# Two mixtures' routing decided inside the self-attention stage ahead of each

## The chip, the cores and the metric

The kernel runs as one program on one core of a Trainium2 chip. Its engines are TensorE (PE, matmul; PEld is its weight load), VectorE (DVE), ScalarE (ACT), GpSimd (POOL) and SyncE (SP, which issues transfers). The metric is the time of one execution in microseconds; lower is better.

## The reference, cut to what matters

A stream `x` of 128 sequences of 32 tokens and 128 channels (4096 tokens, 32 tiles of 128 tokens) passes twelve residual layers. Layers 4 and 5 are a cross-attention and a causal self-attention, layer 6 a mixture of 8 experts with two experts a token and a capacity of 1280 tokens an expert; layer 11 is a causal self-attention with rotary places and layer 12 begins with a second one of its kind and ends in a mixture with one expert a token. For each mixture:

```
logits = norm(x) @ W_router                 # 8 numbers a token
top1   = argmax(logits)                     # or the two best, with softmax weights
u      = norm(x) @ W1[top1] + b1            # GELU with four blocks, or a gated form with two
y      = act(u) @ W2[top1] + b2
x      = x + weight * y                     # weight 0 where the expert is over its capacity
```

What is computed stays the same in the change.

## The kernel before, in words

`X` stays in SBUF as [128, 32 tiles, 128]. The stages run one after another, each a block with a barrier at its end; inside a block each engine has its own ordered list of instructions, and semaphores order them against each other. Three stages are mixtures (`routed_experts`): `a_moe`, `c_moe` (two experts, capacity, four blocks) and `u_moe` (one expert, gated). Before `c_moe` runs `c_self` (`self_attention` with two parts of 32 tiles, so 64 steps), before `u_moe` runs `u_self` (32 steps, rotary, a gate), and after `c_moe` the cross-attention `e_cross`.

**A self-attention** is a software pipeline over steps, one tile a step. `chunk_at(s, place)` says at which step a piece of work for four tiles (a chunk) is due: queries, keys and values before the chunk's first tile, `outputs` at place 7, `output` at 8, the addition onto the stream at 9. Each engine goes through its own list of one step in a fixed order: PE `scores(s)`, projections, `weighted(s-2)`, `turn(s-1)`; DVE `maximum(s)`, `subtract(s)`, `reciprocals`, `unit`; ACT `exponential(s)`, `turned(s-1)`, `apply(s+APPLY)`; POOL `heads(s+2)` and the small arithmetic of the norm (`deviation`). The loop runs to step ALL_TILES + 5.

**A mixture** begins with its front. It cuts the 32 tiles in two halves of 16. DVE takes statistics, POOL the deviation, ACT writes the normed rows (`apply`), PE turns them and forms the logits, DVE chooses experts (`choose`), PE counts with two matmuls, DVE forms each token's row in a buffer sorted by expert (`places`), and POOL scatters every tile's rows to that buffer in DRAM with one indirect DMA a tile and expert (`put(0)`: 32 transfers in `c_moe`, 16 in `u_moe`). Only when the first half is put does SP load sorted tiles (`load`), three at a time, which PE turns (`turn_x`). PE also waits for both halves' owners and, in `c_moe`, for the ranks against the capacity (`s_chosen`); in `u_moe` DVE first adds all of `inner` onto `X`. Then comes the loop over COUNT sorted tiles (78 in `c_moe`, 48 in `u_moe`), each with one expert's weights picked by a register: `up`, activation, `turn_hidden`, `hidden_out`, `down`, `result`. The second half's transfers (`put(1)`) run beside it, one a tile, and the first half's results are fetched back by POOL and added by DVE (`combine`). In `c_moe` the second half's 32 results are fetched in the first 16 tiles of `e_cross` (`fetch_result`, `add_result`).

## Time and profile before

| | us |
|---|---|
| median of 3 runs (lowest, highest) | 4168.02 (4163.99, 4170.11) |
| profiled execution, its own time | 4170.86 |
| profiled execution, span of the trace | 4169.1 |

| stage of the trace | from, us | to, us |
|---|---|---|
| c_self | 1756.7 | 1959.2 |
| c_moe, to the first sorted tile on PE | 1959.5 | 2044.9 |
| c_moe, loop | 2044.9 | 2250.1 |
| e_cross | 2252.7 | 2795.5 |
| u_self | 3779.0 | 3991.5 |
| u_moe, to the first hidden tile on PE | 3991.8 | 4048.5 |
| u_moe, loop and fetching | 4048.5 | 4162.3 |

Times of the trace count from the start of its span. The columns of each view are said at the first group of its rows. A busy share is an average over a stretch: which wait ends last in the stretch is read from the instructions in order of time.

### The profile page before, as it was taken

Reading aid. Unit: us, or ns where it says so; the run is one execution under the profiler, and the core shown is the slowest. Engines: PE = TensorE matmul, PEld = TensorE weight load, DVE = VectorE, ACT = ScalarE, POOL = GpSimd, SP = SyncE. Lnnn points to the kernel's source line nnn. Section 1 sums busy time; section 2 is a strip of 40 time slices with the busy share of each in tenths; the row PEclk is TensorE's granted clock in tenths of the full one; section 3 lists DMA queues with packets and bytes.
Section 4 is the critical chain, followed back from the end, with each engine's and each line's share of the span. In section 5 each row is a group of like instructions: output and inputs, shape, how many; then the busy total and the mean of one; then the engine's idle time right before and its main releaser. Section 6 shows DMA issues by size and latency. Waiting matters only on the chain. (4 is left out here: it accounts for less than half of the span.)

```text
span 4169.1 us, 119554 instructions
## 1 busy us (share of the span) xinstructions
PE 3506.7 (84%) x44673; PEld 2455.7 (59%) x44674; DVE 2783.9 (67%) x6958; ACT 2401.5 (58%) x5931; POOL 2497.3 (60%) x2841
## 2 busy tenths in 40 slices
PE   7999959999999669698598899978589999786766
PEld 5666637777677447465366666655356666453444
DVE  6888856666666423476445998876778888763655
ACT  6777735555555334286123777764567777543633
POOL 6666657767666553475424777655456666755733
PEclk9999979999999779898699999998689999887968
DMA  2111010000000122101121111110011111000023
GB/s 70 35 35 38 27 67 5 7 10 10 6 7 2 51 63 80 50 17 43 51 72 59 46 40 36 38 62 3 2 43 32 38 32 33 2 2 6 2 85 93
DMA packets 90544, 145.87 MB, mean 35 GB/s; under 512 B 10112, under 2 KB 66816, under 8 KB 89664
## 3 DMA queue, kind: packets, MB, share of 16 engines
q1 hardware_dynamic: 79936, 119.72, 8.9%
q0 software_dynamic: 10240, 20.99, 1.6%
q8 instruction: 261, 4.28, 0.4%
q14 instruction: 107, 0.88, 0.1%
HBM read 109.61 MB, written 31.06 MB: 34 GB/s over the span
## 5 line engine op out<-in xcount | busy, mean ns | idle before, releaser
L2230 POOL TENSOR_TENSOR t_cross_E<-t_cross_E,t_cross_inverse 128x1028 f32<-128x1028 f32 x128 | 243.4, 1902 | 164.0 <-DVE t_cross_inverse L2512 164.0
L2230 POOL TENSOR_TENSOR a_cross_E<-a_cross_E,a_cross_inverse 128x1028 f32<-128x1028 f32 x128 | 243.3, 1901 | 157.1 <-DVE a_cross_inverse L2512 157.1
L2230 POOL TENSOR_TENSOR e_cross_E<-e_cross_E,e_cross_inverse 128x1028 f32<-128x1028 f32 x128 | 243.6, 1903 | 137.1 <-DVE e_cross_inverse L2512 136.6
L3063 PE MATMUL l_psum<-l_ffn_w,l_hidden 128*128 128x128 f32 x1536 | 214.9, 284 | 3.0 <-POOL l_hidden L2936 3.0
L3063 PEld LDWEIGHTS l_psum<-l_ffn_w,l_hidden 128*128 128x128 f32 x1536 | 192.3, 193 | 29.9 <-issue 22.2
L3056 PE MATMUL l_psum<-l_hT,l_ffn_w 128*128 128x512 f32 x384 | 204.1, 634 | 0.9 <-ACT l_hT L3120 0.9
L2500 DVE TENSOR_REDUCE t_cross_negtop<-t_cross_psum 128x2 f32<-128x514 f32 x256 | 165.5, 688 | 48.9 <-PE t_cross_psum L2314 47.4
L2500 DVE TENSOR_REDUCE a_cross_negtop<-a_cross_psum 128x2 f32<-128x514 f32 x256 | 165.2, 687 | 40.9 <-PE a_cross_psum L2309 40.4
L2500 DVE TENSOR_REDUCE e_cross_negtop<-e_cross_psum 128x2 f32<-128x514 f32 x256 | 164.9, 685 | 36.5 <-PE e_cross_psum L2309 35.8
L2915 POOL TENSOR_SCALAR l_normed<-inner,l_moments,l_rstd 128x128 f32<-128x128 f32 x192 | 175.6, 924 | 14.8 <-POOL l_rstd L2909 14.8
L3219 DVE TENSOR_TENSOR inner<-l_psum,inner 128x512 f32<-128x512 f32 x48 | 33.2, 692 | 213.0 <-PE l_psum L3048 213.0
L3040 PEld LDWEIGHTS l_psum<-l_qT,l_ctx 32*32 32x32 f32 x6144 | 66.9, 107 | 148.0 <-issue 142.4
L2926 POOL TENSOR_TENSOR l_q<-l_q,l_q_stat 128x512 f32<-128x512 f32 x48 | 50.9, 1060 | 168.6 <-DVE l_q_stat L3199 168.6
L2367 PE MATMUL e_cross_psum<-const_sb,e_cross_E 128*128 128x128 f32 x1024 | 134.0, 274 | 2.7 <-POOL e_cross_E L2230 2.1
L2367 PE MATMUL a_cross_psum<-const_sb,a_cross_E 128*128 128x128 f32 x1024 | 133.7, 274 | 2.2 <-POOL a_cross_E L2230 2.1
L2367 PE MATMUL t_cross_psum<-const_sb,t_cross_E 128*128 128x128 f32 x1024 | 132.8, 273 | 2.1 <-POOL t_cross_E L2230 2.1
L2936 POOL TENSOR_TENSOR l_hidden<-l_hidden,l_less 128x512 f32<-128x512 f32 x96 | 123.1, 1301 | 18.4 <-ACT l_hidden L3144 18.4
L2435 ACT ACTIVATE t_cross_kT<-t_cross_psum,t_cross_weights 128x257 f32<-128x257 f32 x128 | 61.0, 477 | 126.2 <-PE t_cross_psum L2293 126.2
L2435 ACT ACTIVATE e_cross_kT<-e_cross_psum,e_cross_weights 128x257 f32<-128x257 f32 x128 | 61.0, 477 | 121.8 <-PE e_cross_psum L2293 121.8
L2435 ACT ACTIVATE a_cross_kT<-a_cross_psum,a_cross_weights 128x257 f32<-128x257 f32 x128 | 61.0, 477 | 120.5 <-PE a_cross_psum L2293 120.5
L2452 ACT ACTIVATE e_cross_E<-e_cross_psum,e_cross_negtop 128x257 f32<-128x257 f32 x256 | 118.8, 473 | 13.4 <-DVE e_cross_negtop L2500 13.1
L1491 POOL DMA_INDIRECT slots<-hT_all,behind_place_i x64 | 62.0, 968 | 96.6 <-PE c_moe_psum L1623 72.4
(757 smaller groups left out, 11855.6 us busy)
## 6 DMA issues: line engine op xcount, KB each, us to landing
a_cross_context<-context SPq DMA_DIRECT2D x32, 546.0 KB, 3.5
e_cross_context<-context SPq DMA_DIRECT2D x32, 546.0 KB, 3.5
t_cross_context<-context SPq DMA_DIRECT2D x32, 546.0 KB, 3.5
u_moe_weights<-pack_u_moe SPq DMA_DIRECT2D x1, 5633.0 KB
slots<-l_blank SPq DMA_DIRECT2D x6, 832.0 KB, 12.2
a_moe_x_slots<-slots SPq DMA_DIRECT2D x26, 192.0 KB
slots<-a_moe_y_slots SPq DMA_DIRECT2D x26, 192.0 KB
c_moe_x_slots<-slots SPq DMA_DIRECT2D x26, 192.0 KB
```

Source lines behind the costliest of these rows:

```text
L1491: pool.indirect_dma_start(slots.halves[g], bass.IndirectOffsetOnAxis(ap=place_i[:, k, at:at + 1], axis=0), rows[:, at], None).then_inc(s_p ...
L2230: pool.tensor_tensor(E[:, n % N], E[:, n % N], spread(inverse[:, n % 4], SK, 2), ALU.mult).then_inc(s_unit, 1)
L2367: last = pe.transpose(psum[:, (T_BANK, K_BANK)[c], g * P:(g + 1) * P], E[:, n % N, g, c * P:(c + 1) * P], ident)
L2435: act.activation(kT[:, n % 2], psum[:, K_BANK, 0:SK], ACT.Identity, bias=w("bk")).then_inc(s_k, 1)
L2452: act.activation(E[:, n % N, g], psum[:, g, 0:SK], ACT.Exp, bias=negtop[:, n % 2, g:g + 1], accum_out=total[:, n % 2, g:g + 1]).then_inc(s ...
L2500: dve.tensor_reduce(negtop[:, n % 2, at], psum[:, at, 0:SK], AX.X, ALU.max, negate=True).then_inc(s_top, 1)
L2915: last = pool.tensor_scalar(Y1[:, t], c.tile(t), moments[:, 0, t, 0:1], rstd[:, 0, 1, t:t + 1], ALU.subtract, ALU.mult)
L2926: pool.tensor_tensor(groups, groups, spread(q_stat[:, 2], DH, 2), ALU.mult).then_inc(s_soft, 1)
L2936: pool.tensor_tensor(hidden[:, f], hidden[:, f], less[:, f - 2], ALU.add).then_inc(s_late, 1)
L3040: last = pe.matmul(psum[rows, C_BANK, b * S:(b + 1) * S], ctx[rows, b], qT[rows, b * S:(b + 1) * S], start=True, stop=True)
L3056: pe.matmul(psum[:, U_BANKS[f % 2]], c.ffn(f * P), hT2[:], start=True, stop=True).then_inc(s_up, 1)
L3063: last = pe.matmul(psum[:, D_BANK, t * P:(t + 1) * P], hidden[:, f, t * P:(t + 1) * P], c.ffn((NF + f) * P), start=(f == 0 and t == 0), st ...
```

## The change

- The mixture's front becomes two classes: `Choice` (its buffers) and `Front` (its work in pieces, each called by an engine). `self_attention` takes a `choice` and calls the pieces at places 9 (statistics), 10 (deviation), 11 (apply), 13 (turn) and 14 (logits) for chunks 0 to 6; chunk 7 stays in the mixture's stage. The loop of steps goes on to ALL_TILES + 9.
- The first part's choice is made on DVE at steps CHOOSE.. (54, 55 in `c_self`; 26 in `u_self`), the counts on PE at TALLY (57; 28), the places on DVE in three steps from TALLY.
- From step PUT (61; 30) POOL issues one scatter transfer a step: 9 of `c_moe`'s and 8 of `u_moe`'s. The mixture's stage opens with the others.
- The first part of `c_moe` is 12 tiles and not 16 (24 transfers), the second 20 (40 transfers). With the rounding of parts to triples the loop has 81 tiles, not 78. `u_moe` keeps 16 and 16, and 48. `e_cross` fetches 40 results, not 32, over 20 tiles.
- Chunk 7's front, the second part's choice, counts and places, the ranks against the capacity, the weights of the two experts and the addition of `inner` (in 8 pieces) go between the tiles of the mixture's loop. PE no longer waits for `s_chosen`.
- The second part's transfers wait for `s_down` at a pace set so that they end 6 tiles before the first part does.
- Router and expert weights are fetched in the self-attention. The owners' registers are loaded at tile 13 of 16, not 2. `base(c)` on POOL moves from place 5 to place 1 in every self-attention.
- `a_moe` keeps its front in its stage, through the new classes.

```diff
@@ self_attention
+        F_STATS, F_DEVIATION, F_APPLY, F_TURN, F_LOGITS = 9, 10, 11, 13, 14
+        if choice:
+            front = Front(sc, choice, 0, 0)
+            CHOOSE = (ALL_CHUNKS - CHUNKS) * TPC + choice.cut[1] - TPC + F_LOGITS
+            TALLY = CHOOSE + choice.K + 1
+            PUT = max(TALLY + 2, ALL_TILES - 3)
+            choice.ahead_of_stage = ALL_TILES + 6 - PUT
-            for s in range(-STATS, ALL_TILES + 6):
+            for s in range(-STATS, ALL_TILES + (10 if choice else 6)):
@@ POOL, step
-                c = chunk_at(s, 5)
+                c = chunk_at(s, 1)
                 if c is not None:
                     base(c)
+                c = fronted(s, F_DEVIATION)
+                if c is not None:
+                    front.deviation(pool, link, c)
+                if choice and PUT <= s < ALL_TILES + 6:
+                    if s == PUT:
+                        pool.wait_ge(front.s_place, 1)
+                    front.put(pool, slots, 0, s - PUT)
@@ PE, step (after scores and projections, before weighted(s - 2))
+                c = fronted(s, F_TURN)
+                if c is not None:
+                    turned_free(s)
+                    front.turn(pe, c, psum[:, T_BANK])
+                c = fronted(s, F_LOGITS)
+                if c is not None:
+                    front.arrived(pe)
+                    outputs_free(s)
+                    ...
+                    front.logits(pe, c, psum[:, O_BANK, LOGITS])
+                if choice and s == TALLY:
+                    front.tallies(pe, 0, psum[:, O_BANK, TALLIES])
@@ PE, turn(s)
+                c = fronted(s + 1, F_TURN)
+                if c is not None:
+                    pe.wait_ge(front.s_fT, c + 1)
@@ ACT, step (rotary: before powers(c), normed_out(c) and exponential(s))
+                c = fronted(s, F_TURN)
+                if c is not None and rotary:
+                    front.turned(act, c, psum[:, T_BANK])
@@ DVE, step
+                c = fronted(s, F_LOGITS)
+                    ...
+                    front.read_logits(dve, (c,), psum[:, O_BANK, LOGITS])
+                if choice and s == TALLY:
+                    front.places(dve, link, 0, 0, psum[:, O_BANK, TALLIES])
                 if tile_exists(s - 2):
                     unit(s - 2)
+                if choice and 0 <= s - CHOOSE < choice.K:
+                    front.choose(dve, link, 0, s - CHOOSE)
+                if choice and 0 < s - TALLY < 3:
+                    front.places(dve, link, 0, s - TALLY, psum[:, O_BANK, TALLIES])
+                c = fronted(s, F_STATS)
+                    ...
+                    front.statistics(dve, c)
@@ Choice
+        self.cut = 0, first, TILES
+        self.triples = [-(-(self.K * (self.cut[g + 1] - self.cut[g]) + self.E - 1) // 3) for g in range(2)]
@@ routed_experts, POOL
+                    if g == 1:
+                        pool.wait_ge(s_down, PUT_AT + n * (ONE - 6 - PUT_AT) // transfers if begun else n + 1)
+            if begun:
+                for n in range(choice.ahead_of_stage, choice.width(0) * K):
+                    front.put(pool, slots, 0, n)
+                front.deviation(pool, link, LAST)
@@ routed_experts, DVE
+            def beside(i):
+                if i == 2:
+                    front.read_logits(dve, (LAST,), psum[:, COUNT_BANK, 0:TPC * E])
+                if 2 <= i < 2 + K:
+                    front.choose(dve, link, 1, i - 2)
+                if 0 <= i - PLACES_AT < 3:
+                    front.places(dve, link, 1, i - PLACES_AT, psum[:, COUNT_BANK, TPC * E:])
+                ...
+                if capacity and 0 <= i - RANK_AT - 2 < 2 * RANKING:
+                    ranking(*divmod(i - RANK_AT - 2, RANKING))
+                if base is not None and 0 <= i - RANK_AT < CHUNKS:
+                    add_base(i - RANK_AT)
@@ fourth, second_self
+                choice = Choice(sc, "u_router", "top1", inner, hT_rows, "eps6", rms=True)
+                choice = Choice(sc, "c_router", "capacity", X, hT_rows, "eps5", affine=False, first=12)
```

## Rows read from the trace of the kernel before

**Rows 1.** By stretch: PE, PEld, DVE, ACT, POOL busy; TensorE clock, DMA share, GB/s.
```profile
1860.00:1945.00 85.00, 81.41 (x2306) 51.74 (x2306) 68.18 (x180) 70.60 (x132) 61.08 (x76) 1.00 0.02 4
...
1959.50:2045.00 85.50, 25.46 (x113) 23.63 (x114) 40.12 (x172) 17.15 (x41) 44.02 (x64) 0.54 0.22 83
...
3910.00:3975.00 65.00, 52.76 (x1139) 30.28 (x1138) 42.89 (x83) 42.68 (x66) 40.46 (x40) 0.95 0.01 3
...
3991.80:4048.00 56.20, 27.96 (x111) 23.54 (x111) 29.08 (x128) 17.88 (x43) 25.48 (x32) 0.50 0.36 139
4048.00:4137.00 89.00, 83.28 (x421) 55.39 (x421) 62.61 (x158) 41.00 (x111) 30.55 (x32) 0.97 0.28 82
```

**Rows 2.** In order of time, c_moe's front: start, us, what [idle before <-releaser].
```profile
1958.49 0.69 DVE L793 TENSOR_TENSOR X<-c_self_psum,X 128x512 f32<-128x512 f32 x1 [3.09 <-PE c_self_psum L552]
...
2030.09 0.96 POOL L1491 DMA_INDIRECT slots<-hT_all,behind_place_i  x1 [0.30 <-issue]
...
2032.34 13.86 SPq L1433 DMA_DIRECT2D c_moe_x_slots<-slots  x5
...
2044.93 0.87 PE L1592 MATMUL c_moe_psum<-const_sb,c_moe_x_slots 128*128 128x128 f32 x3 [19.15 <-issue]
```

**Rows 3.** The first sorted tiles in a_moe: ns min/median/max, first and last start us.
```profile
L1592 PE MATMUL a_moe_psum<-const_sb,a_moe_x_slots x78: 272/273/476, 1504.9 to 1686.4; 128*128 128x128 f32 x78
L1433 SPq DMA_DIRECT2D a_moe_x_slots<-slots x26: 360/488/1055, 1502.5 to 1665.2; - x26
```

**Rows 4.** In order of time, u_moe's front.
```profile
3990.81 0.69 DVE L793 TENSOR_TENSOR inner<-u_self_psum,inner 128x512 f32<-128x512 f32 x1 [2.17 <-PE u_self_psum L552]
...
4042.31 0.88 PE L1592 MATMUL u_moe_psum<-const_sb,u_moe_x_slots 128*128 128x128 f32 x3 [6.23 <-issue]
...
4040.89 4.42 DVE L1837 TENSOR_TENSOR X<-X,inner 128x4096 f32<-128x4096 f32 x1
...
4048.52 0.69 PE L1614 MATMUL u_moe_psum<-const_sb,u_moe_hidden 128*128 128x128 f32 x2 [0.62 <-DVE u_moe_hidden L1880]
```

**Rows 5.** In order of time, PE: two chunks of c_self, and c_moe's logits.
```profile
1906.56 1.16 PE L552 MATMUL c_self_psum<-c_self_weights,c_self_aT 128*128 128x128 f32 x8
...
1917.60 1.16 PE L552 MATMUL c_self_psum<-c_self_weights,c_self_aT 128*128 128x128 f32 x8
...
1967.17 1.72 PE L1530 MATMUL c_moe_psum<-c_moe_router,c_moe_fT 128*128 128x8 f32 x8
```

**Rows 6.** In order of time, DVE: choice's first, places' first and last instruction.
```profile
1976.29 0.29 DVE L1317 TENSOR_REDUCE c_moe_best<-c_moe_l 128x16 f32<-128x128 f32 x1
...
1982.17 0.29 DVE L1777 COPY c_moe_counts<-c_moe_psum 128x128 f32<-128x128 f32 x1 [1.37 <-PE c_moe_psum L1544]
...
1987.91 0.18 DVE L1796 CAST c_moe_owner_i<-c_moe_owner 128x39 int32<-128x39 f32 x1
```

**Rows 7.** In order of time, c_moe's loop: PE three tiles apart, DVE between two tiles.
```profile
2100.73 1.02 PE L1606 MATMUL c_moe_psum<-c_moe_weights,c_moe_xT 128*128 x2
...
2108.22 1.02 PE L1606 MATMUL c_moe_psum<-c_moe_weights,c_moe_xT 128*128 x2
...
2105.47 0.29 DVE L1897 COPY c_moe_y_slots<-c_moe_psum 128x128 f32<-128x128 f32 x1 [1.36 <-PE c_moe_psum L1623]
```

**Rows 8.** In order of time, u_self: ACT's load for a chunk's powers, PE's `turn_normed`.
```profile
3939.81 1.28 ACT L641 ACT_TABLE_LOAD   x1
...
3939.69 0.66 PE L467 MATMUL u_self_psum<-const_sb,u_self_normed 128*128 128x128 f32 x4
```

**Rows 9.** Adding a fetched result: ns min/median/max, in c_moe and in e_cross.
```profile
L1907 DVE SCALAR_TENSOR_TENSOR X<-behind_got,behind_part,X x32: 342/344/344, 2167.5 to 2245.9; 128x128 f32<-128x128 f32 x32
L2554 DVE SCALAR_TENSOR_TENSOR X<-behind_got,behind_part,X x32: 962/1388/1998, 2283.2 to 2543.3; 128x128 f32<-128x128 f32 x32
```

**Rows 10.** Busy time of POOL's work on e_cross_E, with fetches and without.
```profile
2300.00:2400.00 100.00, 46.64 (x31) 1.00 0.13 41
...
2640.00:2740.00 100.00, 49.69 (x32) 1.00 0.13 39
```

More of the change, by code:

```diff
@@ L336, in _ @@
                 fetch(sp)
+            if choice:
+                front.fetch(sp)
             for c in range(ALL_CHUNKS):
@@ L680, in step @@
                         work(c)
+                c = fronted(s, F_TURN)
+                if c is not None:
+                    front.turned(act, c, psum[:, T_BANK])
                 if tile_exists(s):
@@ L836, in step @@
                             rotate(c, n)
+            link = Link(dve, front.s_link, 0) if choice else None
             steps(step)
@@ L1345, in routed_experts @@
-def routed_experts(core, name, router, rows, slots, kind, choice, nf, source, eps, rms=False, twice=False, capacity=None,
-                   base=None, hT_all=None, store_out=None, behind=None):
-    nc, X = core.nc, core.X
-    E, K, HALF = 8, (1 if choice == "top1" else 2), TILES // 2
-    NT = core.half_tiles[K]
-    TRIPLES = -(-NT // 3)
-    COUNT, LOT = 2 * 3 * TRIPLES, 16
-    halves = kind in ("silu", "glu")
-    width = nf * P * (2 if halves else 1)
+        self.s_put, self.puts = [ctx.enter_context(nc.semaphore(f"put{g}")) for g in range(2)], [0, 0]
@@ new lines, in __init__, with routed_experts @@
+        self.s_got, self.gots = [ctx.enter_context(nc.semaphore(f"got{n}")) for n in range(4)], 0
+def routed_experts(core, name, slots, kind, nf, choice, begun=False, base=None, store_out=None, behind=False):
+    nc, X = core.nc, core.X
+    E, K, cut, rows, hT_all = choice.E, choice.K, choice.cut, choice.rows, choice.hT_all
+    TRIPLES, COUNT, LOT = sum(choice.triples), choice.count, 16
+    ONE = 3 * choice.triples[0]
+    capacity = 1280 if choice.kind == "capacity" else None
+    width = nf * P * (2 if kind in ("silu", "glu") else 1)
@@ L1394, in routed_experts @@
+        front = Front(sc, choice, LAST, 1) if begun else Front(sc, choice, 0, 0)
+        w, arrived, fetch = sc.weights(choice.expert if begun else name)
+        ex = sc.sb("ex", [P, TILES])
+        if capacity:
+            rank1, rank2, tot, tot_b = [sc.sb(n, [P, TILES, E]) for n in ("rank1", "rank2", "tot", "tot_b")]
         x_slots, xT = sc.sb("x_slots", [P, 4, 3, P]), sc.sb("xT", [P, 2, 3 * P])
@@ L1494, in take @@
-            def take(g):
-                stores_done(pool, (g + 1) * TRIPLES)
-                for t in range(HALF):
-                    for k in range(K):
-                        at = g * HALF + t
-                        n = at * K + k
+            link = Link(pool, front.s_dev, 0)
+            def put(g):
+                pool.wait_ge(front.s_place, g - front.g0 + 1)
+                transfers = choice.width(g) * K
+                for n in range(transfers):
+                    if g == 0 and n in (4 * K, 8 * K):
+                        front.deviation(pool, link, PART + 1 + n // (4 * K))
+                    if g == 1:
+                        pool.wait_ge(s_down, PUT_AT + n * (ONE - 6 - PUT_AT) // transfers if begun else n + 1)
+                    front.put(pool, slots, g, n)
@@ L1500, in take @@
+            def take(g):
+                stores_done(pool, choice.triples[0] + g * choice.triples[1])
+                for t in range(cut[g], cut[g + 1]):
+                    for k in range(K):
+                        n = t * K + k
                         if n >= 4:
@@ L1539, in _, with ranks @@
                         turn(c + 1)
-                    choose(c)
-                pe.wait_ge(s_mask, g + 1)
-                mask = flat((one if K == 1 else p8)[:, of(g)])
-                for n, table in enumerate(("upto", "ones")):
-                    last = pe.matmul(psum[:, COUNT_BANK + g, n * P:(n + 1) * P], core.const(table), mask, start=True, stop=True)
-                last.then_inc(s_count, 1)
-            if choice == "capacity":
-                for k, chosen in enumerate((one, two)):
+                    at = c % PART * TPC * E
+                    front.logits(pe, c, psum[:, LOGIT_BANK + g, at:at + TPC * E])
+                front.tallies(pe, g, psum[:, COUNT_BANK + g])
+            arrived(pe)
+            def ranks():
+                for k, chosen in enumerate((choice.one, choice.two)):
                     for n, table in enumerate(("upto", "ones")):
@@ L1580, in load_owners @@
                 if first < last:
+                    if begun and first < ONE < last:
+                        pe.wait_ge(front.s_owner, 1)
                     at = lot % 2 * LOT
@@ L1629, in _ @@
             up(0)
+            if begun:
+                front.turn(pe, LAST, psum[:, RANK_BANK])
             for i in range(COUNT):
@@ L1723, in _ @@
                     hidden_out(i)
+                if begun and i == 0:
+                    front.turned(act, LAST, psum[:, RANK_BANK])
+                if begun and K == 2 and i == RANK_AT:
+                    ratios()
             if shared:
@@ L1814, in _, with apart @@
[L1814 to L1826 removed]
+            def apart():
+                dve.tensor_tensor(ex[:], choice.v2[:], choice.v1[:], ALU.subtract).then_inc(s_apart, 1)
@@ L1857, in load_owners @@
                 if first < last:
+                    if begun and first < ONE < last:
+                        dve.wait_ge(front.s_owner, 1)
                     at = lot % 2 * LOT
@@ L1903, in combine @@
                     dve.wait_ge(s_comb, n)
+                elif n == 0 and base is not None:
+                    dve.wait_ge(s_base, CHUNKS)
                 if K == 1:
```

642 lines of the change are left out of this document (382 added, 260 removed).

## The prediction

> **What bounds the kernel now.** I read the busy shares by stretch first. The reader is to see that no engine is the bound of the whole: PE is busy 96% of a stretch of c_self (81.41 of 85.00) and 81% of one of u_self, but 30% in c_moe's front and 50% in u_moe's, where its clock also falls to about half [rows 1]. In these two fronts the instructions in order of time tell what is waited for. c_moe's lasts from the last addition of c_self (1958.49 + 0.69 = 1959.2) to the first sorted tile on PE at 2044.93: 85.7 us [rows 2]. POOL issues 32 scatter transfers in it, each 0.96 with 0.30 ahead of it, so 1.26; the last ends at 2031.05 [rows 2], and the rest are the ranks, which PE waits for. u_moe's lasts from 3991.5 to the first hidden tile at 4048.52: 57.0 us, with 16 transfers and at its end the 4.42 of DVE's addition of `inner` [rows 4]. The loops behind them run without gaps on PE: three tiles of c_moe take 2108.22 - 2100.73 = 7.49 us [rows 7]. So the fronts are worth 142.7 us together, and what is put in other stages lands where PE or a ring of engines is full.
>
> **What goes.** c_moe's stage opens with 24 - 9 = 15 transfers: 14 x 1.26 + 0.96 = 18.6. SP's load followed the last of them by 1.3 (2032.34 against 2031.05) [rows 2], and in a_moe, where PE waits for nothing else, the first tile came 2.4 after that load (1504.9 against 1502.5) [rows 3]. With 0.5 for the barrier: 22.8, so 62.9 go. u_moe's opens with 16 - 8 = 8: 7 x 1.26 + 0.96 = 9.8, in all 14.0 to the first tile on PE. From there to the first hidden tile it was 6.2 (4042.31 to 4048.52) with DVE held by the addition until 4045.3 [rows 4]; without it, but with chunk 7's rows ahead on ACT, I take 5.2. 57.0 - 19.2 = 37.8 go. **Gain: 100.7.**
>
> **What comes into c_self.** PE gets for each of chunks 0 to 6 four transposes (about 0.44) and eight matmuls for the logits. Eight matmuls of the shape took 1.72 at half clock; eight of 128 columns take 1.16 at the full one, 0.99 to the next [rows 5], so I take 0.9. Two chunks of that place stand 11.04 apart on a full PE [rows 5]; five front chunks fall there, two in the tail. To the 1.3 I add 0.5, because `turn(s-1)` now waits until ACT has emptied the bank: 5 x 1.8 = 9. Bounds: 5 (only the matmuls, and some in idle PE time) and 13.5 (a whole step of 2.7 each). Choice and places on DVE took from 1976.29 to 1988.09 with 1.4 of waiting for PE between them, 10.4 for 16 tiles [rows 6]; for 12 with a copy more I take 9.7, over five steps in which DVE idles 0.2 of 2.76 each [rows 1], so 2.7 hide: 7 stay (0 to 9.7). The tail: chunk 6's rows wait for the addition of chunk 6, POOL's deviation, ACT, PE, and end after chunk 7's output; and POOL's nine transfers and the clearing of semaphores, once done long before the end, end there too. I take 5 (2 to 8). POOL's queue: the transfers begin after the last `heads` is issued, so no tile waits for them; the deviation (1.7) stands ahead of a later `heads`, which POOL issues two steps early (5.5 us): nothing. If that lead is used up, the next scores are late by the rest.
>
> **DVE beside POOL.** One row speaks against putting a choice beside busy POOL: adding a fetched result takes 0.34 in c_moe's loop, where POOL issues transfers, and 0.96 to 2.00, median 1.39, in e_cross, where POOL runs arithmetic on SBUF [rows 9]. In c_self POOL is busy 61.08 of 85.00 [rows 1]. About 17 of the 35 instructions of choice and places read two SBUF tensors, each standing to lose up to 1.05, but they come in bursts of 2 to 4 us in which POOL has one or two instructions; I take 3 for c_self and 2 for u_self (0 to 13 and 0 to 7). **c_self: 9 + 7 + 3 + 5 = 24.**
>
> The Trainium skill (SBUF — State Buffer, Who interferes with whom) says that a DVE instruction with two SBUF inputs contends with a GpSimd instruction that reads SBUF, and that the later one is blocked fully, not slowed. The trace agrees with it where it has such pairs (1.39 against 0.34). By that rule each hit would cost the rest of a POOL instruction, which is a rival below.
>
> **What comes into u_self.** PE, DVE and ACT are busy 81%, 66% and 66% [rows 1], and the chunk of 18 us is a ring of waits. In ACT's list `front.turned` stands ahead of `powers`, `normed_out` and `exponential`. The powers' table load began at 3939.81 [rows 8]; PE's `turn_normed` of that step ran from 3939.69 to 3940.3 [rows 8], and the front's transposes (0.5) and ACT's emptying of their bank (0.7) come behind it, so ACT would begin the load near 3941.7: 1.9 late, with a queue behind it that PE waits for. I take 2.2 for each of four chunks that meet a rotary one (0 to 4.5, a whole step), 1 for each of the three others, 5 of 7 for choice and places in steps of 2.7 at the end, 2 for POOL as above, 3 for the tail. **u_self: 9 + 3 + 5 + 2 + 3 = 22** (9 to 38).
>
> **What comes into c_moe's loop.** Three tiles more: 7.5 [rows 7]. On the full PE: transposes 0.44, logits 0.9, counts 0.6, ranks 1.8: 3.8. On DVE a tile leaves 1.36 before `result` [rows 7] and about 0.3 more. The pieces are (at 0.36 an instruction for 20 tiles) 2.1, 3.6, 1.8, 3.1 and 1.5 for choice and places, and 14 pieces of the ranks of 0.6 to 2.4; what is over 1.67 sums to 5. Chunk 7's rows ahead of the first activation 1.7, ACT's change of table for one exponential 0.7, one register load more 0.9: 3.3. **19.6** (12 to 30). SP now stands at load 11 until the second part's 40 transfers end: they start at tile 8, 40 x 1.26 = 50 us or 20 tiles, so at tile 28, and PE needs that load at tile 31; the stores queued behind it are due at tile 30. It fits by two tiles.
>
> **The rest.** e_cross: POOL's work on its tile runs 46.64 us of 100 with fetches and 49.69 without [rows 10]; with 7.9 of it a tile that is 17.0 and 16.0 us, two fetches a tile, so 0.5 each, eight more: **4** (0 to 8). u_moe's loop: DVE is busy 62.61 of 89.00 [rows 1], 0.55 free a tile; choice, places and eight additions are 11.8, of which 4.8 hide over 12 tiles, and PE gets 1.8: **9** (3 to 14). a_moe: a copy more, **0.3**. `base` at place 1, weights fetched earlier: nothing, both lie beside work with slack.
>
> **Sum.** 100.7 - (24 + 22 + 19.6 + 4 + 9 + 0.3 = 78.9) = 21.8 us less. The profiled execution took 4170.9, so 4149.1 by its own scale; it lies 2.8 above the median shown, against which I give the time: 4168.0 - 21.8 = **4146**. A measurement of this kernel can tell 0.2% from no change, 8.3 us.
>
> **The rivals.** (A) The new pieces hide. For: u_self idles a fifth on every engine, and DVE a fifth in c_self. Then only PE's work stays where PE is full: c_self 9 + 5, u_self 6, c_moe 13, e_cross 4, u_moe 2: 39, time 4168 - 62 = 4106. Against: in-order lists, and bursts of 3 us in steps of 2.7. Chance 0.14.
> (B) Slower. Each front chunk costs a round trip and not its work: PE transposes, waits for ACT to empty the bank before its own `turn`, and ACT's exponential stands behind it. Its price in both self-attentions is up to a step, 2.7 and 4.5, and where choice and logits fall in the same steps the next one is late too. The nine steady chunks stand in my sum with 9 + 9 = 18, 2.0 each; the gain is used up at (18 + 21.8) / 9 = 4.4 each, and at 6 each the time is 4168 + 14 = 4182. For: u_self's ring of waits. Against: c_self's DVE has slack that takes a late step up. Chance 0.10.
> (C) POOL blocks DVE on every instruction with two SBUF inputs: 27 of them x 1.05 = 28 in place of 5, so 4169, no change. For: [rows 9], where no instance was below 0.96. Against: POOL in c_self has gaps and shorter instructions than e_cross's. Chance 0.13. The rule of the skill cited above is this case taken to its end.
> (D) The second part's transfers end late. Each then holds load 11, and PE, directly. At 1.5 us apart and not 1.26 they end at tile 32, the first tile comes 3 tiles late, 8 to 10 us: 4156. Chance 0.08.
> The forecast has 0.55.
>
> **How the numbers follow.** The forecast's own range is 4128 to 4162 (its terms' bounds do not all fall on one side). Faster by over 0.2%, that is below 4159.7: 0.52 of my 0.55, A's 0.14, 0.03 of C's and 0.05 of D's: 0.74. Within: 0.03 + 0.08 + 0.03 = 0.14. Slower: 0.10 + 0.02: 0.12. The range of 8 in 10 leaves half of A and most of B out: 4116 to 4170.
>
> **What would show it.** Right: 9 and 8 transfers on POOL in the tails of the self-attentions, 15 and 8 at the opening of the stages; first sorted tile some 23 and 14 us after the barrier; chunks of c_self in its second half 12.8 apart and not 11.04; c_self's steps 54 to 59 stretched to about 4; 81 tiles at 2.50 with a handful of longer ones among the first 28; PE's clock near full in what is left of the fronts' neighbours. It is wrong if chunks stand further than 15 (B) or not above 11.5 apart (A), if instructions of the choice that took 0.29 take about 1 (C), or if PE waits for a DMA near tile 31 (D).

## The result, and the profile after

The changed kernel takes 4181.08 us (median of 20 runs, 4173.39 to 4190.55) against 4168.44 (20 runs, 4158.0 to 4175.86) beside it: ratio 1.0028, 95% interval 1.0022 to 1.0035. It is slower by 0.28%, some 12 us; forecast were 22 less. The profiled execution took 4184.22 us, with a span of 4182.3 against 4169.1. The experiments add a fact that this pair of numbers hides: the same program, measured again beside `before` on three chips, stood at 0.9982, 0.9963 and 1.0027. The record does not name the chip of the result; it may be the one of the last figure. The chips fall into two kinds by their traces (the last section tells them apart). The account below is for the result's own trace; the last column is one from the other kind.

Stages were cut at the same events in both traces (last instruction of a self-attention, first sorted tile on PE, last row of a mixture), in us:

| term | forecast | before to after | on the chip at 0.9982 |
|---|---|---|---|
| c_moe's front | -62.9 | 85.8 to 24.4: -61.4 | 24.3 |
| u_moe's front | -37.8 | 57.0 to 20.7: -36.3 | 21.0 |
| c_self | +24 | 202.4 to 239.0: +36.6 | 232.3 |
| c_moe's loop | +19.6 | 205.2 to 230.1: +24.9 | 218.6 |
| to the end of e_cross | +4 | 545.4 to 549.8: +4.4 | 550.6 |
| u_self | +22 | 212.5 to 250.2: +37.7 | 240.9 |
| u_moe from its first hidden tile | +9 | 113.8 to 120.8: +7.0 | 120.6 |

With 1.8 at c_self's start and -0.5 between e_cross and u_self that is +14.2 at the last addition. The gains came, within 3 us of 101. The costs are 33 over their sum, all of it in the two self-attentions and the one loop.

The same windows view as [rows 1], of the changed kernel: the second half of c_self, c_moe's front, two chunks of u_self, u_moe's front, and u_moe's loop.
```profile
1866.00:1951.00 85.00, 75.11 (x1987) 49.08 (x1986) 66.55 (x206) 70.03 (x138) 58.86 (x85) 1.00 0.01 3
1997.50:2022.00 24.50, 0.12 (x1) 0.12 (x2) 1.26 (x9) 0.00 (x0) 16.01 (x19) 0.50 0.19 59
3924.00:3978.50 54.50, 42.62 (x670) 25.22 (x664) 30.75 (x73) 31.57 (x54) 28.40 (x32) 0.81 0.01 2
4035.00:4055.70 20.70, 4.88 (x12) 2.48 (x12) 2.71 (x13) 3.50 (x7) 8.92 (x10) 0.51 0.24 73
4055.70:4144.70 89.00, 79.90 (x409) 52.39 (x409) 68.41 (x176) 40.41 (x104) 31.16 (x32) 1.00 0.28 80
```
In c_self PE was busy 96% of such a stretch and is 88%: every engine got work, and none of them is fuller than before. That is the mark of waits, not of a bound. In u_self PE's granted clock is 0.81 where it was 0.95: so nearly two fifths of these 54.5 us go by at 1.2 GHz.

In order of time, the end of c_self and c_moe's front (answers to [rows 2]): the last transfer in the self-attention, its last logits, the first and the last of the stage's 15, SP's load, PE.
```profile
1995.78 0.96 POOL L1658 DMA_INDIRECT slots<-hT_all,c_choice_place_i  x1 [0.30 <-issue]
1997.32 0.19 DVE L1575 TENSOR_TENSOR c_choice_l<-c_self_psum,c_choice_router 128x32 f32<-128x32 f32 x1 [3.78 <-PE c_self_psum L1568]
...
1999.31 0.95 POOL L1658 DMA_INDIRECT slots<-hT_all,c_choice_place_i  x1 [2.57 <-POOLq L168]
...
2016.98 0.96 POOL L1658 DMA_INDIRECT slots<-hT_all,c_choice_place_i  x1 [0.30 <-issue]
2019.23 3.94 SPq L1749 DMA_DIRECT2D c_moe_x_slots<-slots  x5
...
2021.88 0.90 PE L1871 MATMUL c_moe_psum<-const_sb,c_moe_x_slots 128*128 128x128 f32 x3 [24.60 <-DMA c_moe_x_slots<-slots]
```
Transfers stand 1.26 apart and the first tile follows the load by 2.7: the front is what the sum made of it, but for the barrier (1.8 to the first transfer, against 0.5).

In order of time, ACT and PE in a step of u_self that meets front pieces (answers to [rows 8]).
```profile
3923.81 1.26 ACT L1543 ACTIVATE hT_all<-inner,u_choice_factor 128x128 f32<-128x128 f32 x4
...
3929.11 1.09 PE L553 MATMUL u_self_psum<-const_sb,u_self_E 128*128 128x128 f32 x4 [2.25 <-ACT u_self_square L698]
...
3931.92 0.82 PE L1552 MATMUL u_self_psum<-const_sb,hT_all 128*128 128x128 f32 x4
3932.78 0.78 ACT L1560 ACTIVATE u_choice_fT<-u_self_psum,u_choice_router 128x512 f32<-128x512 f32 x1 [1.57 <-PE u_self_psum L1552]
3933.57 1.28 ACT L703 ACT_TABLE_LOAD   x1
...
3936.74 2.07 PE L513 MATMUL u_self_psum<-u_self_hT,u_self_weights 128*128 128x512 f32 x2 [3.60 <-ACT u_self_hT L649]
```
The same two waits of PE in the kernel before, a chunk of 21.8:
```profile
3916.71 0.63 PE L514 MATMUL u_self_psum<-const_sb,u_self_E 128*128 128x128 f32 x4 [1.08 <-ACT u_self_square L636]
3921.53 1.12 PE L477 MATMUL u_self_psum<-u_self_hT,u_self_weights 128*128 128x512 f32 x2 [2.61 <-ACT u_self_hT L587]
```
The ring can be read off. ACT stands at the front's rows for 1.57, and only then loads the table for the powers; PE waits 3.60 for the rows behind them (2.61 before), and then runs at half clock, 2.07 where the pair took 1.12. Ahead of it the four applications (1.26) had pushed the logarithms, for which PE waits 2.25 (1.08 before). A chunk is timed from PE's `output` of the one before it to its own. Chunks 3 and 4, of 21.8, became 27.3: 1.2 from the applications, 2.35 from ACT's stand at the front's rows (1.57 of waiting and 0.78 of work), some 1.4 from the lower clock, and 0.5 is left for PE's new work. This split is a reading of one trace: in `after_again`, `after_third` and `after_fourth`, the same program, chunk 3 took 24.8 at a granted clock of 0.93 and chunk 4 25.9 to 26.0 at 0.87, where both have 27.3 at 0.81 here.

### The profile page after: what moved, and what is told of

It is laid out like the page before. It is cut to its first block and busy times, and to the rows that moved or that the text cites. A ratio compares the mean times of both kernels' runs of the same rounds, so it can differ in the third digit from the quotient of the medians.

```text
span 4182.3 us, 119713 instructions
## 1 busy us (share of the span) xinstructions
PE 3527.8 (84%) x44719; PEld 2461.4 (59%) x44719; DVE 2796.9 (67%) x6989; ACT 2405.0 (58%) x5937; POOL 2494.5 (60%) x2841
## 5 line engine op out<-in xcount | busy, mean ns | idle before, releaser
L2760 DVE TENSOR_REDUCE a_cross_negtop<-a_cross_psum 128x2 f32<-128x514 f32 x256 | 165.1, 686 | 40.4 <-PE a_cross_psum L2569 38.3
L1902 PEld LDWEIGHTS c_moe_psum<-c_experts_weights,c_moe_hT 128*128 128x128 f32 x648 | 80.3, 193 | 74.7 <-issue 74.7
```

The lines of the kernel that those rows point to most:

```text
L1902: last = pe.matmul(psum[:, D_BANK + i % 2, 0:P], hT[:, i % 2, f * P:(f + 1) * P], down_of[:, at, f * P:(f + 1) * P].rearrange("p a c -> p ...
L2760: dve.tensor_reduce(negtop[:, n % 2, at], psum[:, at, 0:SK], AX.X, ALU.max, negate=True).then_inc(s_top, 1)
```

## The experiments

Each is the changed kernel with the edit shown, with its ratio to `before` on the same chip. Five sets ran on four chips: sets 3 and 5 on the same one. "A chip of this kind" means one whose traces look like those of the set spoken of.

**Set 1. One side undone, one place moved.** `u_undone` calls u_self without `choice` and u_moe without `begun=True`; `c_undone` the same for c, with `first` at 16. One part of the change stays in `c_undone`: PE does not wait for the ranks, so its front is 76.2 us and not 85.8.

> The last two stages without the change: u_self has no front pieces, u_moe opens its own stage with all of them (the additions of inner stay beside the expert tiles, where the changed kernel has them). Theory T (the trace of the changed kernel): u_self lost 37.5 us, u_moe's loop 7, its front gained 36, so this kernel is 8 to 9 us under the changed one, about 4172 on the scale of the medians (ratio to before 1.001). Rival R1 (the loss is c's three more tiles and its choice): within 2 of the changed one, 4180. Profile: u_self 3784.8 to about 3997, u_moe's front about 52.

Measured: 0.9975 (0.9966 to 0.9984).

> c_self without front pieces, c_moe with 16 tiles in its first part and 78 expert tiles, all its front in its own stage; u as changed. Theory T: c_self lost 38.3 us (its longer boundary and colder start among them), the loop 24.9, e_cross 3.8, the front gained 61.3, so this kernel is 5 to 6 us under the changed one, about 4175 (ratio 1.002). Rival R1: the whole loss lies here, 4168 (ratio 1.000). Should both undone kernels be at 4168 the two parts do not add up and the trace's accounts are wrong.

Measured: 0.9994 (0.9984 to 1.0004). Both stand further under the changed kernel (by 0.0053 and 0.0034) than the whole of its loss: as this expectation said, accounts that cannot add up. In both, the unchanged side was shorter than in the changed kernel's own trace: `u_undone` has c_moe's loop at 218.7 us and not 230.1. Something other than the edit had changed, and set 2 put the changed kernel itself beside the others.

Laid side by side, the traces of this one chip do price the sides. From u_self's start to the last addition it is 382.4 us with u's side changed (`c_undone`), 379.0 with it undone: as it stands, u's side costs 3.4. From c_self's start to the end of e_cross it is 1025.8 with c's side changed (`u_undone`) and 1028.9 with it undone: 3.1 gained, beside what the ranks already gave.

`u_turn14`, in u_self alone:
```
-        F_STATS, F_DEVIATION, F_APPLY, F_TURN, F_LOGITS = 9, 10, 11, 13, 14
+        F_STATS, F_DEVIATION, F_APPLY, F_TURN, F_LOGITS = (9, 10, 11, 14, 15) if rotary else (9, 10, 11, 13, 14)
```


> u_self's transposes of the front one step later (places 14 and 15 in place of 13 and 14), so that ACT no longer stands at them ahead of the powers' table load, its own rows and the exponential; the same work on every engine, one transfer less ahead of the stage (1.26 us). Theory T (the order in ACT's list costs 2.35 us and a colder PE 0.5 to 1.4 in each of the chunks that meet a rotary one): four to five chunks, so 8 to 14 us less, 4167 to 4173 (ratio 0.999 to 1.001), chunks of 24 us in place of 27.3. Rival R2 (the cost of a chunk is PE's and ACT's added work of 1.4 and 2.0 us with what DVE adds, wherever it stands): 4180 to 4182, chunks of 27.

Measured: 0.9954 (0.9941 to 0.9968), chunks of 24.2. Against the changed kernel on chips of this kind (0.9982, 0.9963) that is 0.001 to 0.003 less, and u_self with its tail is 228.7 us to its last addition where it is 238.7 with the old places on the same chip (`c_undone`). Theory T holds for the whole: the same work one step later is 10 us shorter. Its price for a chunk was too high: on this chip chunks 2 to 5 had been 26.0, 24.9, 26.0 and 19.6, not 27.3, and each got 0.7 to 2.1 shorter.

`c_apply13` has `(9, 10, 13, 14, 15)` in c_self.

> c_self's four applications on ACT two steps later (13 in place of 11; transposes at 14, logits at 15), so that they no longer stand ahead of the step in which ACT brings out the values and the normed rows that the keys wait for. Theory T: the wait of 1.44 us of the keys for those rows goes in each of five to seven chunks, 7 to 10 us less, 4171 to 4174 (ratio 1.001), chunks of 12.6 in place of 14.05. Rival R3 (ACT has as much to do, 11.6 of 14.1 us a chunk, and the wait moves to another step): 4179 to 4182, chunks of 13.8 to 14.1.

Measured: 0.9999 (0.999 to 1.0008), chunks of 13.8. The rival holds. In chunks 10 and 11 the keys' wait of 1.44 was all but gone, and in its place PE waited 1.21 for the four applied tiles before it could transpose them; in chunk 13 the keys' wait was 0.61; the choice now met other pieces, and chunk 14 took 19.9 us. c_self got longer by 6.

**Set 2. The changed kernel again, and three more.**

> The changed kernel once more, beside the others of this study. u_undone and u_turn14 have its c part unchanged, and yet their profiles show c_moe's loop at 218.5 us and c_self's 12.5 for chunk 14, where its own showed 230.1 and 17.0 with waits of PE of 2 to 4 us that nothing in the program explains. If those waits belong to the program (where its instructions lie), ratio 1.0028 and 230 again. If they belong to that chip or that execution, ratio 0.998 to 1.001 and a loop of 218.5.

Measured: 0.9982 (0.9973 to 0.9991). The view of what PE's weight loads and the engines behind them waited for, in the same 20 tiles of c_moe's loop (the 10th to the 29th), in the trace of the result:
```profile
ACT c_moe_hidden L1977 <- PE c_moe_psum L1885: 25.1, 13, 3.9
PEld c_moe_psum L1902 <- issue: 24.7, 21, 3.2
DVE c_moe_y_slots L2147 <- PE c_moe_psum L1902: 21.3, 14, 4.8
```
and on this chip (us in total, times, longest):
```profile
ACT c_moe_hidden L1977 <- PE c_moe_psum L1885: 24.2, 19, 2.0
DVE c_moe_y_slots L2147 <- PE c_moe_psum L1902: 19.4, 18, 3.1
PEld c_moe_psum L1902 <- issue: 15.4, 20, 1.5
```
"issue" is a wait for nothing that the profile shows: 24.7 against 15.4, the longest 3.2 against 1.5. One instance, as DVE sees it, a result that PE had given by its own record 2.3 us before ("remote" is a release that the profile can put down to no engine):
```profile
2062.79 0.29 DVE L2147 COPY c_moe_y_slots<-c_moe_psum 128x128 f32<-128x128 f32 x1 [3.50 <-remote]
```
and the same tile on the other chip:
```profile
2047.12 0.29 DVE L2147 COPY c_moe_y_slots<-c_moe_psum 128x128 f32<-128x128 f32 x1 [1.26 <-PE c_moe_psum L1902]
```

`u14_puts` is u_turn14 with more transfers in the self-attentions' tails, ahead of POOL's wait for the last chunk's statistics (`MORE` is 4 in u_self and 3 in c_self, `MORE_AT` is `ALL_TILES + 1`):
```
+                    first = s - PUT + (MORE if s > MORE_AT else 0)
+                    for n in range(first, first + 1 + (MORE if s == MORE_AT else 0)):
+                        front.put(pool, slots, 0, n)
```


> u_turn14, and in both tails POOL issues more transfers before it waits for the last chunk's statistics (three more in c_self, four in u_self), where it idled 3.75 and 5.90 us. Theory T (the opening of a stage is as long as its transfers): 3 x 1.26 + 4 x 1.26 = 8.8 us less than u_turn14, ratio 0.9933. Rival R4 (the deviation behind the added transfers comes later and with it the last rows and logits, so the tail grows by as much): 0.995 to 0.996.

Measured: 0.9934 (0.9919 to 0.9948), as theory T had it; c_moe's front (counted from c_self's last addition) fell from 28.3 to 24.5 us and u_moe's from 18.9 to 13.8, and the self-attentions kept their length within 1 us.

`u14_warm` is u_turn14 with transposes into columns that nothing reads, before the keys and behind the mean squares, in u_self's steps 8 to 27:
```
+                    if rotary and 8 <= s < TALLY and s % TPC == 1 and place == -7:
+                        for n in range(12):
+                            pe.transpose(psum[:, T_BANK, n % 4 * P:(n % 4 + 1) * P], ident, ident)
...
+                if rotary and 8 <= s < TALLY and s % TPC == 0:
+                    pe.wait_ge(s_O, s - 1)
+                    for n in range(12):
+                        pe.transpose(psum[:, O_BANK, TALLIES.start:TALLIES.start + P], ident, ident)
```


> u_turn14 with work that nothing reads on PE, in u_self's steps 8 to 27 alone: twelve transposes of 128x128 in each of the two waits of a chunk (2.2 us each) that come before the granted clock fell to half. Theory H (part of a chunk's price is PE at half clock after those waits, 6.8 us of each 24): PE stays at the full clock, chunks of 22 to 23 in place of 24.2, 4 to 8 us less than u_turn14, ratio 0.9935 to 0.9945, though PE does more. Rival (the clock is an effect without a price; the added 1.6 us of transposes end later than the waits did): chunks of 24.5 to 26, ratio 0.996 to 0.997.

Measured: 0.9948 (0.9934 to 0.9961). One chunk of u_self in windows, u_turn14 first:
```profile
3904.78:3928.96 24.18, 19.46 (x342) 11.67 (x332) 15.84 (x37) 16.28 (x29) 14.85 (x18) 0.86 0.01 2
```
```profile
3899.90:3922.47 22.57, 20.10 (x365) 13.17 (x356) 15.65 (x37) 16.27 (x29) 14.87 (x18) 1.00 0.01 2
```
PE does more and the chunk is 1.6 us shorter, at a granted clock of 1.00 and not 0.86. Over the kernel the 0.0006 between the two is inside their intervals; by the chunks theory H holds, and u_self is 226.3 us to its last addition for 228.7. The clock fell to 1.2 GHz behind PE's two waits and rose when PE was kept at work. (The Trainium skill, TensorE: Matmul & The Clock Gate, Part 1, says that the throttled state is the default and that activity releases it; by that rule, the trace agrees.)

`u_apply14` has `(9, 10, 14, 15, 16)` in u_self.

> As u_turn14, but the four applications on ACT too in the step with the least on ACT (places 14, 15 and 16 for applications, transposes and logits), two transfers less ahead of the stage than in the changed kernel (2.5 us). Theory T: the applications (1.27 us) stood ahead of the values, the exponential and the logarithms, whose table load PE waits for 2.25 us; 1.2 less in each of six chunks, 7 less than u_turn14, less 1.3 for a transfer: ratio 0.994. Rival R2 (ACT has as much to do): 0.9955 to 0.996.

Measured: 0.9955 (0.9942 to 0.9969). Chunks 3 and 4 fell to 22.2 and 22.9 us, below u_turn14's, but chunk 5, which meets the choice, rose to 21.1 from 17.9, and the missing transfers cost 2 in u_moe's front. The rival's number, though its reason (no room on ACT) fits neither chunk 3 nor 4, which gained 2.0 and 0.9.

**Set 3. On a chip of the result's kind.**

> The changed kernel a third time: it stood at 1.0028 of before where its result was taken and at 0.9982 (0.9973 to 0.9991) beside the second set of experiments, with 27 us less in the profile, 11.4 of them in c_moe's loop and 4.7 in one chunk of c_self, where PE had waited 2 to 4 us at a time. If 0.9982 is what the program gives and the first was a peculiarity of that chip: 0.998 to 0.999 here, a loop of 218.5 us. If the program has two ways to go, the runs of this set fall into two groups, 4150 and 4180.

Measured: 1.0027 (1.0018 to 1.0037), chunk 14 at 17.0 and the loop at 230.3; the 12 runs are one group, 4174.0 to 4189.68. So one program gives both times, and neither alternative of the expectation came: it is the kind of chip, or at least of the set (each set ran on one chip at one time; this chip gave the same in set 5). `before` is touched too, 4169.74 here against 4162.36 in set 2, but less.

`c_fine` records the instructions of `choose` and `places` and gives c_self's DVE three of them a step:
```
-            TALLY = CHOOSE + choice.K + 1
+            TALLY = CHOOSE + (choice.K + 1 if rotary else 5)
...
+                    if s != TALLY:
+                        pieces.run(3 if s < ALL_TILES - 2 else 4)
```


> The changed kernel with c_self's choice and places in pieces of three instructions a step over ten steps, in place of pieces of 5, 10, 6 and 10 over five; the same instructions, the tallies two steps later, three transfers less ahead of the stage (3.8 us). Theory T2 (a piece of 2 to 4.5 us on DVE makes the scores of its step late, a piece of 0.9 hides beside what DVE idles): chunks 12 and 13 of 14.1 to 15 in place of 15.5 and 19.6, c_self 5 us shorter, all in all 1 to 2 us less than the changed kernel, ratio 0.998. Rival (the work itself costs, wherever it stands, as DVE has no room): c_self as long as before or longer, ratio 0.999.

Measured: 1.0015 (1.0006 to 1.0023). The chunk with most of the choice, in windows, in the trace of the result and in c_fine:
```profile
1946.57:1966.27 19.70, 13.44 (x319) 9.09 (x311) 17.18 (x53) 10.78 (x22) 8.29 (x11) 0.91 0.01 2
```
```profile
1946.65:1961.95 15.30, 12.91 (x320) 8.86 (x311) 14.46 (x40) 10.71 (x22) 8.34 (x11) 1.00 0.01 3
```
DVE's work in it fell by 2.7 (spread over more chunks), the chunk by 4.4. Against `after_third` on the same chip c_self is 8.1 shorter to its last addition, but 2.5 of that lies in chunks 4 and 5, which the edit does not touch, and its start is 2.0 longer. Theory T2 holds for the chunks (14.2 and 15.3 in place of 15.4 and 19.7). Over the kernel it is 0.0012 less, net of 2.6 us for the transfers, with the two intervals overlapping: a gain of 0 to 8 us.

`c_late_weights` lets SP wait for the last chunk's values (`sp.wait_ge(s_vp, ALL_CHUNKS)`) before it fetches the experts' 4 MB.

> The changed kernel with the fetch of the experts' weights (at 370 to 420 GB/s for some 10 us) issued only when the last chunk's values are projected, near 1955, in place of chunk 4. Theory W (the bulk transfer is what made chunk 4 take 13.0 to 15.0 us in place of 11.47 in every kernel with c's part, and 11.50 without it): chunk 4 takes 11.47, the stretch with the transfer is 2 longer at most where PE waits in any case, 1 to 3 us less in all, ratio 0.9975 to 0.998. Rival (chunk 4 is slow for another reason): chunk 4 stays at 13 to 15.

Measured: 1.0026 (1.0017 to 1.0035). Chunk 4, in after_third and here:
```profile
1832.92:1847.63 14.71, 11.99 (x320) 7.47 (x311) 10.11 (x29) 11.36 (x21) 10.81 (x15) 0.98 0.73 290
```
```profile
1827.51:1838.98 11.47, 11.38 (x320) 7.13 (x311) 9.12 (x27) 9.60 (x19) 8.30 (x12) 1.00 0.02 6
```
At a DMA share of 0.73 the chunk was 3.2 longer, and without the transfer it is 11.47 again: theory W holds for the chunk. The time did not follow (1 to 3 us less were expected): the transfer now ran beside the choice, and no gain can be told from none.

> u14_puts and u14_warm together. If their gains over u_turn14 add up (0.0020 and 0.0006), ratio 0.9928, u_self 226 to 228 us with its tail; if the added transposes cost what they gain by the clock, 0.9934 as u14_puts.

Measured: 0.9988 (0.9979 to 0.9997), on this kind of chip, where the changed kernel stands at 1.0027. u_self was 232.1 to its last addition, c_self's chunks 14 and 15 19.8 and 9.1: with three more transfers beside them they got longer by 2.8 and 1.7 than in after_third. That points at the transfers. Against the changed kernel of this kind it is 0.0039 less; the two expected ratios were for the other kind, and whether the gains add up stays open.

**Sets 4 and 5. The transfers taken away, and the best of all.** Set 4 fell on a chip of the other kind.

> The changed kernel beside the three others, to name the kind of chip: 0.998 of before with chunk 14 of c_self at 12.3 us and c_moe's loop at 218.5, or 1.003 with 17.0 and 230. A value between them would say that there are not two kinds.

Measured: 0.9963 (0.9949 to 0.9976), chunk 14 at 12.1, loop 219.5.

`c_no_puts` sets `PUT = ALL_TILES + 6` in c_self, so that none of the nine transfers is issued there.

> The changed kernel with no transfer of c_moe's first part in c_self: all 24 open the mixture's stage, nine more than before this edit (11.3 us there). Theory P (PE is held while POOL issues indirect transfers, on one kind of chip): there chunk 14 falls from 17.0 to 12.3 and chunk 15 from 7.4 to 6.1, so 11.3 - 6 = 5 us more than the changed kernel (ratio + 0.0012); on the other kind both stay and it is 11 us more (+ 0.0027). Rival (chunk 14 is long because of the clock or of chunk 13): 17.0 stays on the first kind, and 11 us more on either.

Measured: 1.0004 (0.9994 to 1.0014), 0.0041 over after_fourth, where 0.0027 was expected; chunk 14 at 11.8. c_self and the front together are 10.2 us longer (11.3 expected), the rest lies in stages that the edit does not touch. There is no pause here to take away; set 5 got the other kind.

> c_no_puts once more. If c_moe's loop is 230 us, the chip is of the kind on which the changed kernel stood at 1.0028 and 1.0027, and theory P expects chunk 14 of c_self at 12 us and a ratio of 1.004, its rival 17.0 and 1.006. If the loop is 219, it repeats what is known: 11.8 and 1.000 to 1.001.

Measured: 1.0026 (1.0017 to 1.0035), loop 231.6. In order of time on PE, the output of chunk 13 and of chunk 14, after_third first and c_no_puts2 second, both on the same chip:
```profile
1969.84 2.08 PE L591 MATMUL c_self_psum<-c_self_weights,c_self_aT 128*128 128x128 f32 x8
1986.88 1.44 PE L591 MATMUL c_self_psum<-c_self_weights,c_self_aT 128*128 128x128 f32 x5
```
```profile
1962.91 2.08 PE L593 MATMUL c_self_psum<-c_self_weights,c_self_aT 128*128 128x128 f32 x8
1975.23 0.94 PE L593 MATMUL c_self_psum<-c_self_weights,c_self_aT 128*128 128x128 f32 x6
```
17.0 against 12.3 us. In after_third this falls beside POOL's transfers. POOL issues four in a row between 1979.7 and 1984.6, DVE waits 3.03 for a result of PE, and PE 4.16 for what ACT makes of its transposes:
```profile
1981.08 0.96 POOL L1658 DMA_INDIRECT slots<-hT_all,c_choice_place_i  x1 [0.30 <-issue]
...
1983.61 0.96 POOL L1658 DMA_INDIRECT slots<-hT_all,c_choice_place_i  x1 [0.30 <-issue]
1985.51 0.26 DVE L861 RECIPROCAL c_self_inverse<-c_self_psum 128x16 f32<-128x16 f32 x1 [3.03 <-remote]
1986.24 0.71 PE L568 MATMUL c_self_psum<-v_own,c_self_ET 128*32 128x36 f32 x32 [4.16 <-ACT c_self_ET L683]
```
Theory P holds for c_self's tail: take the transfers out, and the pause is gone, at about the same granted clock (0.82, and 0.80 in after_third). Chunk 13 is not the reason either: it took 19.7 here and in the trace of the result, where chunk 14 took 17.0. Its number did not come: 1.004 was expected, its rival's was 1.006, and 1.0026 is below both. c_self and the front together are 265.7 us here and 266.5 in after_third, though c_self's start, which varies with one program, is 2.8 shorter here. So on this kind of chip the nine transfers put ahead of the stage bring no gain that can be told from none (1.0026 without, 1.0027 with); on the other they are worth the 10.2 us above. PE's own record has its transposes done at 1982.1, 3.5 us before ACT takes them up: whether PE stood, or its results were late to be seen, the profile does not tell.

`best` is c_fine, u_turn14, the late fetch and u14_puts with `MORE` at 4 and 2; `best_warm` adds the transposes.

> c_fine, u_turn14, the late fetch of the weights and the packed transfers of u14_puts (four in u_self, two in c_self, where the places are known later). The parts gave, each against the changed kernel of its kind of chip: 0.0012, 0.0028, 0.0001 and some 0.0015: 0.0056 together, so 0.9926 of before on the one kind of chip and 0.9971 on the other; where they share a gain, 0.001 less.

Measured: 0.9937 (0.9923 to 0.995); 0.0011 short of the sum of its parts.

> best and the transposes that nothing reads in u_self's waits, which gave 0.0006 over u_turn14: 0.9920 or 0.9965; if the clock has no price of its own, no gain over best, or a loss of up to 3 us where the added work ends later than the wait.

Measured: 0.9926 (0.9912 to 0.9939), 4.4 us by the medians under `best`; u_self is 226.3 to its last addition for 229.8. The clock has a price of its own.

> best_warm once more: 0.9926 on the kind of chip with a loop of 219 us. On the other kind, where the changed kernel stands 0.0045 to 0.0065 higher against before, 0.997 to 0.999.

Measured: 0.9961 (0.9947 to 0.9975) on a chip of the result's kind, below the 0.997 to 0.999 that were expected. This version beats both kernels on either kind, by 0.4% and 0.7% of `before`.

## Why the prediction was wrong

The step that failed is "what comes into u_self", 22 where it was 37.7, with c_self (36.6 for 24) and c_moe's loop (24.9 for 19.6) behind it. What the runs show in its place: a piece put ahead of other work in ACT's list delays, in that step, everything that PE waits for behind it, and PE then works on at half clock. By its own steps:

- **The gain** (100.7) was 97.7. Right: transfers and load as the rows had it; the barrier takes 1.8 and not 0.5.
- **"2.2 for each of four chunks that meet a rotary one"**: +5.2, +5.5, +5.6 and +5.1 (on one chip of the other kind, `c_undone` against `u_undone`: +5.4, +4.2, +5.7 and +5.1). The place was right, ACT's list ahead of the powers, and its size there too (1.9 expected, 2.35 found). What was left out is the four applications ahead of the logarithms (1.2), PE's clock (0.95 to 0.81 in that stretch) and that the three last chunks are in the same ring: "1 for each" were +9.2, +3.9 and a tail of 3. Rival B had this mechanism, at a chance of 0.10; it priced the ring by work and waits alone. u_turn14 and u14_warm show the order and the clock, by 10 us of u_self and by 1.6 a chunk; u_apply14 the applications, by 2.0 and 0.9 in chunks 3 and 4, some of it again by the clock.
- **c_self, "5 x 1.8 = 9"**: two chunks met only rows and logits, and took +3.0 and +3.1: 1.5 of PE's work, as expected, and 1.44 of PE waiting for rows that ACT brings out behind the four applications, where the sum had 0.5 for another wait. Five such chunks are 15. That the applications' place is the cause is not shown: c_apply13 moved them, the wait turned into one of 1.21 for the applied rows, and a chunk got only 0.3 shorter. What a better order on ACT would give stays open. DVE's statistics of a chunk, 1.7 us in one step, stood in no term.
- **Choice and places, "7 stay"**: chunks 12 and 13 grew by 4.4 and 8.65, which is 7 over the 3.0 of such a chunk. The size was right, the reason not: it was reckoned from DVE's room over five steps, but c_fine gave 5.6 of it back by the size of the pieces alone.
- **c_self's start**, in no term: +3.5 to the first chunk's output. PE's clock rose later (0.76 granted over the first 41.5 us, before 0.88 over 38.3). That is no part of the change: over all traces this stretch took 36.6 to 41.4 us, also with one program.
- **"weights fetched earlier: nothing"**: 1.5 to 3.5 us in chunk 4, in every run but those with the late fetch and c_undone, which has no early one.
- **POOL's transfers beside PE**, costed at nothing: right on the one kind of chip, wrong on the other. Between after_again and the trace of the result lie 4.7 in chunk 14, 1.3 in chunk 15, 11.5 in the loop and 3 in u_self's chunk 6, together about 20 of the 35 us between the two traces (27 between the medians); 4 more are the clock in u_self's chunks 3 and 4. That decides the sign: 0.9982 and 0.9963 on the other kind of chip, and the prediction's range (0.9875 to 1.0005 of before) holds those. Even there the gain, 0.0018 and 0.0037, is short of the 0.0052 forecast. Only c_self's part of it is tied to the transfers by an experiment.
- **The loop, 19.6**: 24.9 here, on the other kind 13.4 and 14.3 over `before` (12.1 and 13.0 over c_undone's 206.5). The work was priced too high, the pauses not at all.
- **e_cross 4, u_moe's loop 9**: 4.4 and 7.0. Right.
- **C**: on three of some 17 instructions with two SBUF inputs, not on all; two of them, at 1.0 where c_choice_cand's addition beside them took 0.32:
```profile
1959.01 0.97 DVE L1622 TENSOR_TENSOR c_choice_first_tile<-c_choice_tiles_upto,c_choice_tiles_of 128x8 f32<-128x8 f32 x1
1960.01 1.07 DVE L1622 TENSOR_TENSOR c_choice_ahead<-c_choice_upto,c_choice_counts 128x96 f32<-128x96 f32 x1
```
Some 2.2 us where 3 were taken; in c_fine three others were held. **D** did not come: load 11 went out at 2115.3, and the tiles from 30 on stand 2.5 apart (two of 3.2 apart). **A** is excluded by every chunk that meets the front.

## What to carry to other kernels

Price a piece that is put into an in-order pipeline by the step that it lands in: what stands behind it in that engine's list, who waits for that, and whether the piece is longer than that one step's room; sums of work over a stage gave about half of a chunk's price here. Cut it to the room of a step, and keep it off the step with the table load. Where PE begins to wait, count its next instructions at half clock; and measure a change of half a per cent on more than one chip before its sign is believed.

## What was not expected of the hardware

- The traces fall into two kinds, with nothing between. a_moe's last part (from its last sorted tile's result to PE's last instruction), in which POOL issues indirect transfers one behind another and which the change leaves as it was, takes 42.6 to 44.1 us in the twelve traces from three chips, and 48.5 to 55.0 in the other eight: those of `before` and of the result, and six from the chip of sets 3 and 5. `before` is 6 to 11 us slower on that chip too.
- In c_moe's loop the two kinds part in every second tile from the 10th to the 26th, and by most at 10, 12 and 18 (5.6, 5.9 and 5.0 us, against 2.5, 4.2 and 2.5). Through all of that stretch POOL issues two or three transfers a tile without a break. The old loop, with one a tile and a wait between, is as long on either kind: 205.2 us in `before` and 206.5 in `c_undone`. So the pauses go with rows of transfers. In c_self an experiment shows the transfers to be their cause; in the loop none was made. What in the chip differs stays open. The Trainium skill (SBUF — State Buffer, Who interferes with whom) says that "PE and ACT never wait on anyone". It says so of the ports of SBUF; no run here shows whether these results of PE are held at a port or elsewhere, only that they come up to 3 us late.
- A transfer of 4 MB, at a DMA share of 0.70 to 0.81 over the chunk, made chunk 4 of c_self 1.5 to 3.5 us longer on either kind of chip, with PE waiting 0.8 to 2.3 for "issue" in the middle of 32 matmuls that needed nothing from DRAM.
- Work that nothing reads made u_self faster: 12 transposes in each of two waits, chunks of 22.57 in place of 24.18.
